# Splitting the four score banks of an attention block: two for query rows, two for transposed tiles

## What is computed

```
x = x + 0.5 * ffn(layernorm(x))      # dense 4096x4096 plus a routed low-rank part
x = x + attention(layernorm(x))      # 32 heads, causal, latent q and kv, rotary half
x = x + 0.5 * ffn(layernorm(x))
```

```
scores = q @ k.T * scale             # 2048 x 2048, causal
attn   = softmax(scores, axis=-1)
out    = attn @ v
```

## Time and profile before

| what | value |
|---|---|
| median of three runs | 9008.8 us (9007.5 to 9396.88) |
| time of the profiled execution | 9008.8 us |
| span in its trace, slowest core (7) | 9007.2 us |
| the other cores' spans | 8962.8 to 8998.0 us |
| stage of the heads, about | 2243 to 6343 us of the span |
| PE, DVE, ACT busy over the span | 74%, 26%, 13% |

### The profile page before, as it was taken

One profiled execution on the slowest core, in us unless ns is written; L12 is line 12 of the kernel. 1 busy time (PEld: TensorE's weight loads), 2 busy tenths in 40 slices (PEclk: granted clock), 3 DMA queues, 4 the chain that ended last, 5 costly groups with the idle time before them and its releaser, 6 DMA issues.

```text
span 9007.2 us, 77692 instructions; the slowest of 8 cores (8962.8 to 9007.2 us)
## 1 busy us (share of the span) xinstructions
PE 6650.2 (74%) x25940; PEld 2473.0 (27%) x25940; DVE 2354.2 (26%) x4285; ACT 1148.4 (13%) x1974; POOL 222.3 (2%) x423
## 2 busy tenths in 40 slices
PE   3289996285777777777777777777587887249999
PEld 1134442132222222222222222222233333014444
DVE  3410002501333333333333333333000001520000
ACT  0000000001222222222222222222000000000000
POOL 0000000000000000000000000000000000000000
PEclk7699998687777777777777777777788988669999
DMA  5046666011000000000000000000433334203333
GB/s 85 0 114 147 148 149 116 12 26 35 6 8 8 8 6 8 8 8 6 8 8 8 6 8 8 8 6 6 124 84 84 86 84 90 48 10 112 112 110 106
DMA packets 205068, 453.73 MB, mean 50 GB/s; under 512 B 27601, under 2 KB 49490, under 8 KB 204306
## 3 DMA queue, kind: packets, MB, share of 16 engines
q0 software_dynamic: 59840, 177.65, 11.3%
q1 hardware_dynamic: 135634, 237.57, 8.6%
q10 hardware_dynamic: 9216, 33.56, 1.4%
HBM read 440.44 MB, written 152.31 MB: 66 GB/s over the span
## 4 chain that ended last, share of the span: by engine, by line
PE 67%; DVE 16%; DMA 7%; issue 6%; ACT 2%; DVEq 1%; SPq 0%; ACTq 0%; POOL 0%; POOLq 0%
PE scores L586 10%; PE scores L1256 6%; PE scores L1462 5%; PE scores L1248 5%; DVE Cf L1348 4%; PE pbA L1275 4%; DVE lgf L1361 3%; PE pbC L1162 3%; PE pbD L1263 3%; PE pbA L586 2%; PE pbB L586 2%; PE pbD L586 2%; PE pbC L586 2%; DMA Ff<-fw_wo 2%; PE scores L1215 2%
## 5 line engine op out<-in xcount | busy, mean ns | idle before, releaser
L1361 DVE TENSOR_REDUCE lgf<-scores 128x1 f32<-128x512 f32 (+3 forms) x1280 | 709.9, 605 | 1841.0 <-PE scores L1215 1306.5
L1312 ACT ACTIVATE A<-scores 128x512 bf16<-128x512 f32 x1280 | 764.6, 597 | 1553.4 <-PE scores L1256 1551.4
L586 PE MATMUL scores<-A,Ff 128*128 128x512 bf16 x4096 | 889.3, 379 | 0.0
L1215 PE MATMUL scores<-A 128*128 128x512 bf16 (+3 forms) x1280 | 442.7, 398 | 390.0 <-DVE lgf L1361 388.0
L1248 PE MATMUL scores<-A 128*128 128x512 bf16 x1280 | 621.6, 486 | 44.3 <-ACT Ff L1304 31.1
L1256 PE MATMUL scores<-Ff,onesr_bf 1*128 1x512 bf16 x1280 | 604.3, 472 | 0.0
L1275 PE MATMUL pbA<-A 128*128 128x512 bf16 x1280 | 583.6, 456 | 11.6 <-DVE ctxstg L1352 11.5
L1462 PE MATMUL scores<-A,Ff 128*128 128x512 bf16 x2048 | 481.0, 400 | 114.9 <-DMA Ff<-fw_wo 114.9
L586 PEld LDWEIGHTS scores<-A,Ff 128*128 128x128 bf16 x4096 | 400.8, 98 | 483.3
L1183 PE MATMUL pbC<-A 128*64 128x512 bf16 x256 | 132.1, 620 | 317.4 <-DVE A L1336 237.9
L354 ACT ACT_TABLE_LOAD x3 | 3.8, 1283 | 2654.3 <-DVE rowA L328 2654.3
(11 more groups left out here) (233 smaller groups left out, 6492.0 us busy)
## 6 DMA issues: line engine op xcount, KB each, us to landing
Cf<-x0t SPq DMA_DIRECT2D x128, 256.0 KB, 4.2
Ff<-fw_base POOLq DMA_DIRECT2D x64, 512.0 KB, 7.4
basebf<-Ff POOLq DMA_DIRECT2D x64, 512.0 KB, 4.7
x1t<-Cf SPq DMA_DIRECT2D x128, 256.0 KB, 6.0
Cf<-x1t SPq DMA_DIRECT2D x128, 256.0 KB, 3.5
Ff<-fw_wo POOLq DMA_DIRECT2D x64, 512.0 KB, 8.4
x2t<-Cf SPq DMA_DIRECT2D x128, 256.0 KB, 3.9
Cf<-x2t SPq DMA_DIRECT2D x128, 256.0 KB, 3.3
```

The lines of the kernel that those rows point to most:

```text
L586: i = te.matmul(banks[c] if ob % 2 else banks[c][:, 0:512], Ff[:, (si % 2) * 2048 + k * 128:(si % 2) * 2048 + (k + 1) * 128], A[:, dglob * ...
L1215: mmi = te.matmul(sl[:, 0:N], A[:, qf(h) + i * 128:qf(h) + (i + 1) * 128], A[:, kf(h) + kc:kf(h) + kc + N], start=True, stop=not diag)
L1312: ns.sG.inc(se.activation(pts(GT), SB4[SLOTMAP[("T", h, J, tau)]][:, 0:512], AF.Exp))
L1361: ns.sVs.inc(ve.reduce_max(ns.lgf[:, L_NM + par * 4 + k:L_NM + par * 4 + k + 1], SB4[SLOTMAP[("q", h, i, k)]][:, 0:N], axis=AX, negate=True))
```

## The change

The list of blocks is split in two. The q blocks alternate between banks 0 and 1, the T blocks between banks 2 and 3; each block waits for the one two places back in its own list. No instruction is added, removed or moved on any engine; only the banks and the values that PE waits for differ.

```
-    BLKS = [ev for ev in TEVS if ev[0] in ("q", "T")]
-    SLOTMAP = {ev: ix % 4 for ix, ev in enumerate(BLKS)}
-    GUARDB = {ev: (BLKS[ix - 4] if ix >= 4 else None) for ix, ev in enumerate(BLKS)}
+    QB = [ev for ev in TEVS if ev[0] == "q"]
+    TB = [ev for ev in TEVS if ev[0] == "T"]
+    SLOTMAP = {ev: ix % 2 for ix, ev in enumerate(QB)}
+    SLOTMAP.update({ev: 2 + ix % 2 for ix, ev in enumerate(TB)})
+    GUARDB = {ev: (QB[ix - 2] if ix >= 2 else None) for ix, ev in enumerate(QB)}
+    GUARDB.update({ev: (TB[ix - 2] if ix >= 2 else None) for ix, ev in enumerate(TB)})
```

## The result

| | kernel before | changed kernel |
|---|---|---|
| median of 12 runs | 9202.7 us | 9371.1 us |
| lowest | 9007.5 us | 9236.8 us |
| ratio, changed to before | | 1.0267, 95% interval 1.0201 to 1.0333 |

The medians hold runs in which the cores of one die or both were granted a lower clock, which happens to either kernel; the ratio comes from the runs without it, as do the times of other kernels further down, while the profiles of the changed kernel, `after_again`, `q3_t4`, `after_fill06` and `inter_shared` come from runs with it. On the profiled 9008.8 us of before the ratio stands for 9249 us. The change made the kernel slower by 240 us. The forecast was 156 us (9165): right in sign, too small by a third. The "slower by over 2%" that came had been given 0.31.

The account below looks back on a forecast made before the run. PE and DVE take turns, DVE pacing q sections and PE the drains. Losses of 1.05 + 1.56 + 2.31 + 0.18 = 5.10 us a head, 163 us for 32, gave 9172; with clock steps 9165 was taken, range 9075 to 9275.

Parts of the forecast that it names:

- slower by over 2%: Whole kernel: the outcome of a measured time more than 2% above the kernel before; chance 0.31.
- PE's lead at their ends: Ends of q sections: PE leaves with one or two reductions still to do, instead of up to three or four.
- The four latencies: q sections: 0.60 us between reduction starts, 0.28 between rows, 0.48 matmul to reduction, 0.84 reduction start to released q matmul.
- T(t+2)'s wait for the exponential: Body of every drain: exponential t is ready in time, by a small margin at worst, so the wait costs nothing.
- The 0.11 us set down for T2 in drain 0: Drain 0: T2 newly waits for the first exponential, 1.81 us after T0 against 1.70, so 0.11 more.
- The drains themselves should last as now: All drains: their lengths stay unchanged; drains that stretch would show the prediction wrong.
- Place A, rows 0 to 6 and drain 0, warm by then: Rows 0 to 6 and drain 0, at the warm clock: T0 0.94 us later, T2 0.11 more, 1.05 a head.
- the first rival: Drain 1 or 2: one more cold stretch in each head, 3.1 us on top of 5.1, 9271 us; chance 0.26.
- the second rival, the good clock: Shifted drains meet the short form in every head, saving 1.7 us a head, 9118 us; chance 0.13.
- the 0.03 that the prediction had named as a sign of being wrong: Drains 1 and 2: a granted clock moving by more than 0.03 over many heads would show the prediction wrong.
- The argument from steps in a head's length: Whole head: lengths come in steps of about 3.1 us, the next being 132.6 or up to 133; 9152 to 9165 us.
- the prediction read it as 9009: Whole kernel: two banks satisfy the rule of rotating matmul groups through different PSUM banks, so the time stays at 9009 us.

Follow-up runs that it names:

- after_again: The changed kernel run once more with no edit: 9233.7 us, beside 9003.5 of the kernel before.
- q3_t4: Against the kernel before, q blocks rotate over banks 0 to 2, T blocks over all four: 9174 to 9182 us on one die, about 1.02.
- after_fill06: The changed kernel plus an unread 512-column matmul ahead of each q block of rows 3 to 6: 9165, 9170 and 9215 us on one die.
- inter_shared: The kernel before, four banks kept, PE's list putting rows 7, 8, 11, 12 and 15 between tiles of drains 0 to 2: 8578.5 us, 0.952.
- q2_t4: Against the kernel before, only the q blocks are limited to banks 0 and 1, T blocks rotate over all four: 9247.3 us.
- q4_t2: Against the kernel before, q blocks keep four banks, T blocks alternate between the two used longest ago: 9022.7 us beside 9003.5 and 9015.0.
- q2_rows06: Against the kernel before, two banks for the q blocks of rows 0 to 6 only, four elsewhere: 9127.3 us (one run).

## Why the prediction was right and wrong

**Right: DVE paces q sections, and PE's lead at their ends is what two banks take away.** The four latencies carried (means over 30 heads below). Rows 0 to 6 lost 1.35 us on average against 0.94 forecast, rows 7 to 10 1.60 against 1.56, rows 11 to 14 2.18 against 2.31, row 15 0.20 against 0.18 (`q2_t4` less before). Together 5.3 against 5.0 us a head. `q4_t2` and `q2_t4` show that it is this and nothing on T's side. The one clear miss, rows 0 to 6, comes mostly from the head that was read: its rows 0 to 6 take 5.98 us, as in 4 of 30 heads, and 26 take some 5.63. From 5.98 the forecast puts T0 at 6.92, and it comes after 7.03 on average.

**Right: what costs nothing.** T(t+2)'s wait for the exponential shows up as 3 us in the whole stage. The 0.11 us set down for T2 in drain 0 could not be seen in the changed kernel, whose drain 0 is cold; `q4_t2`, where it stays warm, has 0.1 in an ordinary head.

**Wrong: the clock.** The failed step is that the cost of the clock in drain 0 was put at nothing ("The drains themselves should last as now"). It stands in two places. "Place A, rows 0 to 6 and drain 0, warm by then" took the clock of before for granted in a section that the change itself made thinner. And the first rival looked for "one more cold stretch" in "drain 1 or 2", where the clock was cold already, and not in drain 0, the one drain that ran wholly warm and so had something to lose. Its argument against, that PE's total idle time between two sections hardly changes, left out the new idle time within rows 0 to 6. Drain 0 lost 3.94 us a head, at a granted clock of 0.59 instead of 1.00.

Drains 1 and 2 gave 0.99 and 0.88 back: drain 1 has its short form (under 15 us) in 23 of 30 heads instead of 14, and drain 2 takes less than 20 us in 15 heads instead of none. That is about what the second rival, the good clock, expected (1.7). Their granted clocks moved from 0.67 to 0.72 and from 0.66 to 0.70, more than the 0.03 that the prediction had named as a sign of being wrong. The net of the clock is about 2.0 us a head (with 0.1 in drain 3), 63 us in all; with 5.3 x 32 = 171 that is 234, and 240 was measured. That the first rival's 9271 lies nearer to 9249 than the forecast's 9165 is in part luck: it had the kind of loss right, but its 3.1 us stood in another drain, and it had no gain to set against them.

The argument from steps in a head's length did not hold either. The heads of before do come at 126.4 and 129.5, those of `q2_t4` at 132.4 to 133.5 (half of them), 137 and 139 to 141: the 133 that the prediction picked is the shortest common form, and taking it for all heads left out the longer ones. The mean was 135.9.

Of the rules weighed there, the Trainium skill's "A second HAM failure mode: psum-queue depth-cycling" (TensorE: Matmul & The Clock Gate), small idles between matmul groups that make the clock swing, was the better guide. The runs bear it out: with fewer banks for the q blocks such idles grew and the clock fell, and in `after_fill06`, with work put into them, drain 0 was warm again at 7.2 us. The other rule of the Trainium skill (Perfetto Trace Analysis, "Matmuls"), rotation through different PSUM banks, names no number of banks; the prediction read it as 9009, and rotation over two was not enough.

**What stays open.** Why the clock recovers earlier in some drains than in others was not settled, nor where `after_fill06` gave the rest of its gain back. The section means are those of `q2_t4`; the changed kernel's own profile (core 3) has 7.03 us for rows 0 to 6 and 10.71 for drain 0.

## What to carry to other kernels

Where two engines take turns, the depth of the buffers between them is not only for steady flow: it is the work that one engine can leave behind for the other when the phase changes. Count it at each phase's end, not in mid-phase. When a change makes TensorE's work thinner, look for the stretch behind it that still runs warm and price it cold (6.95 us became 11.2 here), even where nothing waits in that stretch. And before dividing buffers between two streams that never run at the same time, put the streams side by side: the order was worth 5%, the split cost 3% in either order.

## What was not expected of the hardware

TensorE's clock follows work that is of no use just as well. Seven spare matmuls a head turned drain 0 from 0.59 to 0.98 of 2.4 GHz on average, and a q block computed twenty times over behind a reciprocal took 4.5 us off the drain that follows. A stretch in which PE is busy without a gap can also stay at 1.2 GHz: five microseconds of drain 1 in the changed kernel, PE busy throughout:

```profile
4015.00:4020.00 5.00, 5.00 (x11) 1.10 (x11) 0.00 (x0) 2.84 (x5) 0.00 (x0) 0.50 0.00 0
```

The length of a cold drain is also no constant. Drain 2 takes 21.7 to 24.8 us in the heads of one core of the kernel before, and its mean went from 22.3 to 20.5 in `q2_rows06`, which does not touch it. So differences of up to some 3 us in a section of a single head say little here without a mean over the heads.
